# An attention stage over graph edges: scores spread from two row halves of TensorE, zero-one matrices in bf16, denominator factors written in place by ScalarE

## The reference, cut to what matters

```python
q, k, v = (x @ Wq.T), (x @ Wk.T), (x @ Wv.T)          # each (N, H=8, C=16)
scores = einsum('ehc,ehc->eh', q[dst], k[src]) / sqrt(C) + edge_attr @ We.T
seg_max = segment_max(scores, dst)
ex = exp(scores - seg_max[dst])
denom = segment_sum(ex, dst)
out = segment_sum(v[src] * (ex / denom[dst])[:, :, None], dst)
```

## Time and profile before

| | us |
|---|---|
| median of 3 runs | 6932.62 (6927.31 to 6932.69) |
| profiled execution | 6936.31 |
| its span in the profile | 6934.5 |

### The profile page before, as it was taken

How to read it: one execution, slowest core, us unless ns; L and a number is a source line. 1 busy time by engine, 2 the same in 40 slices (tenths; PEclk the granted TensorE clock), 3 DMA queues, 4 the chain that set the end, 5 groups by cost and what they waited for, 6 DMA issues and landing times. The chain is left out here.

```text
span 6934.5 us, 161023 instructions
## 1 busy us (share of the span) xinstructions
PE 5765.9 (83%) x49778; PEld 3934.9 (57%) x49778; DVE 4671.8 (67%) x15150; ACT 2162.6 (31%) x5294; POOL 3099.4 (45%) x3151
## 2 busy tenths in 40 slices
PE   4699999999998999984566659999889999599996
PEld 2466666666666666663344436666456666366664
DVE  7455555555555555558999967777557777577776
ACT  3222222222222222223333323333443333433332
POOL 1555555555555555547000025555145555355552
PEclk9655555555555555555556679999999999799997
DMA  4333333333333333324222233333343333533335
GB/s 145 116 89 87 88 87 88 88 88 89 87 87 87 88 89 86 89 70 131 86 66 70 65 115 105 106 103 104 102 128 104 104 105 101 163 104 106 106 102 152
DMA packets 542000, 688.39 MB, mean 99 GB/s; under 512 B 217072, under 2 KB 427905, under 8 KB 541722
## 3 DMA queue, kind: packets, MB, share of 16 engines
q0 software_dynamic: 140208, 338.71, 17.1%
q1 hardware_dynamic: 401692, 348.45, 16.6%
HBM read 619.25 MB, written 67.52 MB: 99 GB/s over the span
## 5 line engine op out<-in xcount | busy, mean ns | idle before, releaser
L740 POOL DMA_INDIRECT at_kv<-kv_tab,at_idx x1568 | 1562.2, 996 | 1296.6 <-issue 593.6
L2250 ACT ACTIVATE ag_msg<-ag_pair 128x768 bf16<-128x768 f32 x1200 | 925.9, 808 | 1586.4 <-PE ag_pair L2180 1027.1
L2189 PE MATMUL ag_sum<-ag_hot,ag_msg 128*128 128x240 bf16 x10800 | 1300.5, 268 | 69.6 <-issue 55.5
L2189 PEld LDWEIGHTS ag_sum<-ag_hot,ag_msg 128*128 128x128 bf16 x10800 | 974.6, 98 | 443.3 <-issue 366.6
L2064 POOL DMA_INDIRECT ag_spill<-g_tab,ag_idx x600 | 580.1, 967 | 1429.5 <-DMA ag_idx<-spill_tab 777.8
L2119 DVE CAST ag_msg<-ag_pair 128x768 bf16<-128x768 f32 x600 | 572.9, 955 | 588.8 <-PE ag_pair L2180 277.2
L2180 PE MATMUL ag_pair<-xs,ag_pick 128*32 128x384 bf16 x14400 | 821.3, 331 | 153.4 <-DVE ag_pick L2092 63.0
L2071 POOL DMA_INDIRECT ag_spill<-g_tab,ag_idx x750 | 724.5, 966 | 462.3 <-issue 179.1
L2102 DVE TENSOR_SCALAR ag_hot<-iota_win,ag_node 128x240 bf16<-128x240 bf16 x4350 | 901.2, 290 | 0.0
L989 PE MATMUL at_ps_bc<-at_sct,at_sel_head 64*128 64x128 f32 x3136 | 696.8, 408 | 33.9 <-issue 8.2
L989 PEld LDWEIGHTS at_ps_bc<-at_sct,at_sel_head 64*128 64x128 f32 x3136 | 639.2, 308 | 52.0 <-ACT at_sct L1059 41.1
(11 more groups left out here) (331 smaller groups left out, 9093.9 us busy)
## 6 DMA issues: line engine op xcount, KB each, us to landing
ag_pick<-slot_tab SPq DMA_DIRECT2D x150, 768.0 KB
rk_hi_bc<-hi_tab SPq DMA_DIRECT2D x50, 896.0 KB
at_attr<-attr SPq DMA_DIRECT2D x196, 128.0 KB
at_qd<-q_tab SPq DMA_DIRECT2D x1568, 12.0 KB
at_kv<-kv_tab,at_idx POOLq DMA_INDIRECT x1568
ag_spill<-g_tab,ag_idx POOLq DMA_INDIRECT x1350
tr_dv<-dinv_tab SPq DMA_DIRECT2D x72, 256.0 KB
g_tab<-xs SPq DMA_DIRECT2D x48, 384.0 KB
```

The lines of the kernel that those rows point to most:

```text
L740: nc.gpsimd.indirect_dma_start(kv[:, s.slot, ch, :], None, env["kv_tab"], bass.IndirectOffsetOnAxis(ap=idx[:, s.slot, ch:ch + 1], axis=0)) ...
L2189: last = nc.tensor.matmul(sum_ps[k][:, 0:WIN], row[:, part * DIM:(part + 1) * DIM], hot[:, k, ch, :], start=first and part == 0, stop=end ...
L2250: nc.scalar.activation(msg[:, p % 4, :, :], pair_ps[p % 3][:, :, 0:3 * DIM], ACT.Copy).then_inc(copied[p], 1)
```

## The change

- spread_scores: the turned scores (sct) are now on all 128 partitions, twice the same 64 rows. The heads 0 to 3 are spread from partitions 0 to 63 into ps_bc[0], the heads 4 to 7 from partitions 64 to 127 into ps_bc[1], with the matmuls of the two halves in turn (tile_position row 0 and row 64). Still 8 float32 matmuls. sel_head changes its shape accordingly and is made with two affine_selects.
- turn_scores: the transpose becomes two float32 matmuls with the identity, whose results go to partitions 0 to 63 and 64 to 127.
- bf16: hot, big_c, low_row and ones_row are made in bf16. place stays float32, and ScalarE makes a copy place_b in bf16 (cast_place). turn_hot and turn_place become bf16 matmuls with a bf16 identity (ident16); two of the three matmuls of near_max are bf16.
- denominators: sa_ps and its matmul are gone. ScalarE computes the same exponential a second time, directly into partitions 64 to 71 of scale_d (row 72 stays 1.0), and shrink reads that.
- order: on VectorE place_one and hot_one stand ahead of messages and fall_short, place_one first; on TensorE turn_hot and turn_place stand ahead of sum_up; on ScalarE cast_place stands between copy_scores and gain_exp. New waits: place_cast in near_max and turn_place, den_scale_made in shrink, scaled (of the block before) in scale_exp.

```diff
--- before.py
+++ after.py
@@ -583,13 +583,13 @@
...
         identb = tile("identb", [P, P], BF16)
-        sel_head = tile("sel_head", [C * HEADS, HEADS, P])
+        sel_head = tile("sel_head", [P, HALF, P])
         sel_feat = tile("sel_feat", [HEADS, HC, HEADS])
-        sel_aux = tile("sel_aux", [HEADS + 1, HEADS + 1])
         we = tile("we", [P, G * HEADS])
-        big_c = tile("big_c", [P, HEADS, C])
-        low_row = tile("low_row", [1, HEADS * C])
-        ones_row = tile("ones_row", [1, P])
+        ident16 = tile("ident16", [P, P], BF16)
+        big_c = tile("big_c", [P, HEADS, C], BF16)
+        low_row = tile("low_row", [1, HEADS * C], BF16)
+        ones_row = tile("ones_row", [1, P], BF16)
         turn, wrap, step = tile("turn", [P, 1]), tile("wrap", [P, 1]), tile("step", [P, 1])
@@ -598,18 +598,19 @@
...
 
-        hot = tile("hot", [P, SLOTS, P])
+        hot = tile("hot", [P, SLOTS, P], BF16)
         hot_w = tile("hot_w", [P, SLOTS, C * GAP + W])
...
         place = tile("place", [P, SLOTS, P])
+        place_b = tile("place_b", [P, SLOTS, P], BF16)
         place_t = tile("place_t", [P, SLOTS, P])
...
         sc = tile("sc", [P, SLOTS, C * HEADS])
-        sct = tile("sct", [C * HEADS, 2, P])
+        sct = tile("sct", [P, 2, P])
         ml = tile("ml", [P, HEADS])
@@ -619,7 +620,8 @@
...
         fall = tile("fall", [HEADS, P])
-        scale = tile("scale", [HEADS + 1, P])
+        scale = tile("scale", [HEADS, P])
+        scale_d = tile("scale_d", [P, P])
         m_node = tile("m_node", [P, HEADS])
@@ -631,9 +633,9 @@
...
         mt_ps, back_ps, mbt_ps = ps_max[:, 64:72], ps_max[:, 72:80], ps_max[0:HEADS, 128:256]
-        sf_ps, sa_ps = ps_scale[:, 0:128], ps_scale[AUXD:AUXROWS, 128:256]
+        sf_ps = ps_scale[:, 0:128]
         me_ps, bias_ps = ps_scale[:, 384:448], ps_scale[:, 448:512]
-        hot_ps, place_ps, sct_ps = ps_turn[:, 0:128], ps_turn[:, 128:256], ps_turn[0:C * HEADS, 256:384]
+        hot_ps, place_ps, sct_ps = ps_turn[:, 0:128], ps_turn[:, 128:256], ps_turn[:, 256:384]
         num_ps, den_ps = ps_node[:, 256:384], ps_node[AUXD:AUXROWS, 384:512]
...
@@ -692,22 +695,23 @@
...
             nc.gpsimd.memset(sel_feat[:, :, :], 0.0).then_inc(made, 1)
-            nc.gpsimd.memset(sel_aux[:, :], 0.0).then_inc(made, 1)
             nc.gpsimd.memset(hot_w[:, :, :], 0.0).then_inc(made, 1)
-            nc.gpsimd.memset(scale[:, :], 1.0).then_inc(made, 1)
+            nc.gpsimd.memset(scale_d[:, :], 1.0).then_inc(made, 1)
             nc.gpsimd.memset(msg[:, :, :, MSG - 1:MSG], 1.0).then_inc(made, 1)
...
             nc.gpsimd.memset(turn[:, :], 0.0).then_inc(made, 1)
-            pool.wait_ge(made, 11)
-            nc.gpsimd.affine_select(out=sel_head[:, :, :].rearrange("p h (c w) -> p h c w", w=W),
-                                    in_=sel_head[:, :, :].rearrange("p h (c w) -> p h c w", w=W),
-                                    compare_op=ALU.not_equal, fill=1.0, base=0,
-                                    pattern=[[-1, HEADS], [-HEADS, C], [0, W]], channel_multiplier=1).then_inc(made, 1)
+            pool.wait_ge(made, 10)
+            for j in range(2):
+                pool.wait_ge(made, 10 + j)
+                nc.gpsimd.affine_select(out=sel_head[:, :, :].rearrange("p h (c w) -> p h c w", w=W),
+                                        in_=sel_head[:, :, :].rearrange("p h (c w) -> p h c w", w=W),
+                                        compare_op=ALU.not_equal, fill=1.0, base=-(C * HEADS + HALF) * j,
+                                        pattern=[[-1, HALF], [-HEADS, C], [0, W]], channel_multiplier=1
+                                        ).then_inc(made, 1)
             nc.gpsimd.affine_select(out=sel_feat[:, :, :], in_=sel_feat[:, :, :], compare_op=ALU.not_equal, fill=1.0,
                                     base=0, pattern=[[0, HC], [-1, HEADS]], channel_multiplier=1).then_inc(made, 1)
-            nc.gpsimd.affine_select(out=sel_aux[:, :], in_=sel_aux[:, :], compare_op=ALU.not_equal, fill=1.0, base=0,
-                                    pattern=[[-1, HEADS + 1]], channel_multiplier=1).then_inc(made, 1)
+            nc.gpsimd.tensor_copy(ident16[:, :], ident[:, :]).then_inc(made, 1)
             nc.gpsimd.tensor_scalar(identb[:, :], ident[:, :], BIG, None, ALU.mult).then_inc(made, 1)
@@ -864,12 +868,13 @@
...
                     dve.wait_ge(scale_spread, s.nth)
+                    dve.wait_ge(den_scale_made, s.nth)
                     if not (isinstance(s.n, int) and s.n < 1):
...
                     nc.vector.tensor_tensor(num, num, sf_ps, ALU.mult).then_inc(scaled, 1)
-                    nc.vector.tensor_tensor(den, den, sa_ps, ALU.mult).then_inc(scaled, 1)
+                    nc.vector.tensor_tensor(den, den, scale_d[AUXD:AUXROWS, :], ALU.mult).then_inc(scaled, 1)
 
@@ -882,8 +887,8 @@
...
                     (4, scale_nodes), (4, load_bases), (3, node_max), (2, add_up), (3, load_first), (4, shrink),
-                    (3, raise_max), (2, add_bias), (4, merge), (3, messages), (3, fall_short), (0, hot_one),
-                    (0, place_one)], w)
+                    (3, raise_max), (2, add_bias), (4, merge), (0, place_one), (0, hot_one),
+                    (3, messages), (3, fall_short)], w)
                 dve.wait_ge(added, 2 * (w + 1) * sh.BLOCKS)
@@ -911,9 +916,8 @@
...
                     pe.wait_ge(above_made, s.nth if isinstance(s.n, int) and s.n == sh.BLOCKS - 1 else s.nth + 1)
-                    nc.tensor.matmul(sf_ps, sel_feat[:, :, :].rearrange("h d e -> h (d e)"), scale[0:HEADS, :], start=True, stop=True)
-                    nc.tensor.matmul(sa_ps, sel_aux[:, :], scale[:, :], start=True, stop=True,
-                                     tile_position=(0, AUXD)).then_inc(scale_spread, 1)
+                    nc.tensor.matmul(sf_ps, sel_feat[:, :, :].rearrange("h d e -> h (d e)"), scale[:, :], start=True,
+                                     stop=True).then_inc(scale_spread, 1)
 
@@ -923,9 +927,10 @@
...
                     pe.wait_ge(place_made, s.nth)
+                    pe.wait_ge(place_cast, s.nth)
                     nc.tensor.matmul(near_ps, ones_row[:, :], low_row[:, :].rearrange("p (h c) -> p h c", h=HEADS),
                                      start=True, stop=False, skip_group_check=True)
-                    nc.tensor.matmul(near_ps, place[:, s.slot, :], big_c[:, :, :], start=False, stop=False,
+                    nc.tensor.matmul(near_ps, place_b[:, s.slot, :], big_c[:, :, :], start=False, stop=False,
                                      skip_group_check=True)
@@ -966,7 +971,11 @@
...
                     alone(pe)
-                    nc.tensor.transpose(sct_ps, sc[:, s.slot, :], ident[:, :]).then_inc(sc_turned, 1)
+                    for j in range(2):
+                        at = slice(C * HEADS * j, C * HEADS * (j + 1))
+                        last = nc.tensor.matmul(sct_ps[at, :], sc[:, s.slot, :], ident[:, :], start=True, stop=True,
+                                                tile_position=(0, C * HEADS * j))
+                    last.then_inc(sc_turned, 1)
 
@@ -982,26 +991,28 @@
...
 
-                def spread_scores(j):
-                    def run(s):
-                        pe.wait_ge(sct_made, s.nth)
-                        for h in range(HALF):
-                            last = nc.tensor.matmul(ps_bc[j][:, h * P:(h + 1) * P], sel_head[:, HALF * j + h, :],
-                                                    sct[:, s.slot % 2, :], start=False, stop=h == HALF - 1,
-                                                    skip_group_check=True)
-                        last.then_inc(bc_made[j], 1)
-                    return run
+                def spread_scores(s):
+                    pe.wait_ge(sct_made, s.nth)
+                    for h in range(HALF):
+                        for j in range(2):
+                            own = slice(C * HEADS * j, C * HEADS * (j + 1))
+                            last = nc.tensor.matmul(ps_bc[j][:, h * P:(h + 1) * P], sel_head[own, h, :],
+                                                    sct[own, s.slot % 2, :], start=False, stop=h == HALF - 1,
+                                                    skip_group_check=True, tile_position=(C * HEADS * j, 0))
+                            if h == HALF - 1:
+                                last.then_inc(bc_made[j], 1)
 
...
                     alone(pe)
-                    nc.tensor.transpose(hot_ps, hot[:, s.slot, :], ident[:, :]).then_inc(hot_turned, 1)
+                    nc.tensor.matmul(hot_ps, hot[:, s.slot, :], ident16[:, :], start=True, stop=True).then_inc(hot_turned, 1)
 
                 def turn_place(s):
-                    pe.wait_ge(place_made, s.nth)
-                    nc.tensor.transpose(place_ps, place[:, s.slot, :], ident[:, :]).then_inc(place_turned, 1)
+                    pe.wait_ge(place_cast, s.nth)
```

(18 more changed lines are left out.)

7 lines of the change are left out of this document (4 added, 3 removed).

## The result

The changed kernel takes 6853.52 us (median of 4 runs, 6851.56 to 6858.99) against 6931.14 us for the kernel before (4 runs, 6927.31 to 6932.69): ratio 0.989, 95% interval 0.9873 to 0.9907, 78 us less. Forecast were 6550 us and a range of 6390 to 6800: the direction held, the size was off by 300 us, and the time lies outside the range.

A forecast was written before the change was run, and what follows sets the result against it. TensorE's queue was taken to set the 14.92 us block; edits saving 2.52 gave 12.40, plus 0.90 for a late signal, less 0.6 for the clock, 12.70 us per block. Forecast 6550 us, range 6390 to 6800.

The forecast's parts named there:

- Spreading: Spreading the scores on TensorE: products of the two row halves run side by side, gain 1.71 of 3.72 us per block.
- rival D: Row halves do not run beside each other in float32: 13.85 us per block, 6774 us; 9%.
- near_max: TensorE's near_max products: two go from two float32 records each to one bf16 record, gain 0.55 us (0.4 to 0.8).
- The turns: turn_hot and turn_place on TensorE: one bf16 record each, gain 0.1 us per block (-0.2 to 0.3).
- turn_scores: Transpose of the scores on TensorE becomes two float32 products in four records, costing 0.36 us per block (0.2 to 0.6).
- The held signal: Back-to-back gathers delay turn_near's signal to VectorE's raise_max, adding 0.9 us per block (0.4 to 1.07).
- The clock: TensorE's denser work brings more rises of its clock, saving 0.6 us per block (0 to 1.5).
- Rival C: TensorE's clock stays high for most of the stage and gathers bind at 10.6 us per block, 6137 us; 7%.
- rival E: A second late signal per block costs another 0.9 us: 14.2 us per block, 6843 us; 8%.
- Rival F: Slower: the signal of spreading itself is also late, by 1.8 us: 15.1 us per block, 7019 us; 6%.

The follow-up runs named there:

- e1: The changed kernel with four gathers per block instead of eight, part of the attention left out; 6372.08 us, 0.9273 of the kernel before.
- e7: The kernel before without its pace() line, so eight gathers stand back to back; 6268.63 us against 6262.31 for the kernel before, ratio 1.0006.
- e12: The changed kernel with scores transposed and spread from one row half as before; 6755.76 us against 6932.08 for the kernel before, ratio 0.9747.
- e15: The changed kernel with scores transposed and spread from one row half as before; 6088.15 us against 6263.72 for the kernel before, ratio 0.9724.
- e9: The changed kernel as it is, run again; 6853.99 us where the kernel before takes 6932.08, ratio 0.9887.
- e5: The changed kernel as it is, run again; 5959.45 us where the kernel before takes 6262.31, ratio 0.9513.

## Why the prediction was wrong, point by point

**Which edits are worth what: right.** The sum said 12.40 us of TensorE per undisturbed block; e1's block shows 11.98. Spreading 2.01 us (forecast 2.01), so the row halves run side by side in float32 with their weight loads, and rival D is out. near_max 0.97 us, in e1 0.80 (forecast 1.1). L915 is gone. The turns 0.32 us from L1010 to sum_up at 1505.15 (forecast 0.38). turn_scores 0.82 us to its copy (forecast about 0.75). Most of what the block is shorter than forecast is near_max, whose gain was forecast too small. The Trainium skill ("TensorEngine Tiling (Array Packing)", Key Properties) says that different tiles load weights and multiply in parallel; the 16 records in 2.01 us agree, now for float32 too.

**The held signal: the step that failed.** It was in the sum at 0.9 us per block, as a signal of turn_near, whose reader has slack; with the clock's 0.6 taken off, 0.3 us were to be added to TensorE's own work. Measured are 14.24 - 11.98 = 2.26 us. The term was too small because it had the wrong products in it. With the block shorter the bias and turn_max came into the run, and more of spreading. Readers that started over 1 us later than is usual in their kernel, between 500 and 2300 us, counted on the first engine record that reads the product:

| product | before | the change |
|---|---|---|
| turn_near | 21 of 123 | 27 of 126 |
| bias | 6 of 123 | 71 of 127 |
| turn_max | 6 of 123 | 57 of 127 |
| spreading (starts of run_max) | 47 of 246 | 116 of 254 |
| spread_max | 25 of 122 | 4 of 126 |

I had placed the run by events up to L958 and not asked which product stands next in TensorE's queue if the run lasts six gathers, not five. turn_near, the product that I had in the sum, hardly changed.

What held signals cost in all can be read from the two kinds of groups, the program of a row being the same (of before, e7 stands in for the free group, as it is as fast as before there):

| | held group, block | free group, block | difference |
|---|---|---|---|
| before | 14.66 | 12.57 (e7) | 2.09 |
| one row half | 13.71 (e12) | 11.54 (e15) | 2.17 |
| the change | 14.23 (e9) | 11.00 (e5) | 3.23 |

So the edits are worth 12.57 - 11.00 = 1.57 us per block, 306 us, in a free group, and in a held one 3.23 - 2.09 = 1.14 of it is lost. What is left is 0.43 us, 84 us: the measured gain. The row halves alone give 11.54 - 11.00 = 0.54 us and lose 3.23 - 2.17 = 1.06. These differences hold the waits and the lost rises of the clock together; the runs do not part them.

**The clock: wrong, and bound up with the held signals.** I expected more rises and 0.6 us per block from them. The granted clock stayed at 0.56 (before 0.57). Where nothing is held it is higher for both kernels. The totals of 600 to 2300 us, first e5 (the change), then e7 (before without pace()), the granted clock third from the end:

```profile
600.00:2300.00 1700.00, 1534.74 (x10159) 970.97 (x10158) 1260.97 (x3230) 609.96 (x2461) 1261.29 (x1234) 0.67 0.42 116
...
600.00:2300.00 1700.00, 1621.35 (x9064) 1144.75 (x9064) 1146.39 (x2843) 456.72 (x1894) 1052.96 (x1081) 0.65 0.37 102
```

The same stretch shows 0.57 for both kernels in a held group. In e7 there are two kinds of block and no other: 78 of 143 take 10.5 to 10.7 us, with 6.8 us of it at the raised clock, and 65 take 14.9 at the lower level. Before, in the held group, has 17 short ones of 123, and 41 of over 16 us. So most of what the free group gives the kernel before comes through the clock: my estimate is 1.7 of the 2.09 us, the share of short blocks rising from 14 to 55% at 4.3 us each. And the 0.26 us that I took for the net worth of a rise was the worth with held signals behind it. The change itself did little to the clock, 0.65 to 0.67 in the free groups. Rival C needed the transposes, turned into products, to raise the clock. The Trainium skill ("TensorE: Matmul & The Clock Gate", Part 4) says that a transpose does not count as busy in the way that products do; three per block were turned here, and neither pair of clocks (0.57 and 0.57 held, 0.65 and 0.67 free) shows much of it, though no run turned them alone.

**The rivals.** Nearest came rival E (14.2 us per block, 6843 us), a second held signal per block; it had 8%. That its number fits is in part luck: a held bias came in 71 of 127 blocks, mostly 1.8 to 2.2 us late, and such blocks are 2.1 us longer than the others; it is not 0.9 in every one. Rival F, the sign turned, did not come as a whole, though its mechanism did: starts of run_max, which reads the products of spreading, were late in 116 of 254 cases. And for the row halves alone F's outcome is true in the held group where both ran: with them 6853.99, without them 6755.76.

**The range.** Its upper end took in E only in part. The price for a held signal was taken from one row on a product with slack, and its frequency from one run of gathers. The bound that the rows would have allowed is the full delay on a product without slack, 2.42 - 0.60 = 1.82 us: 12.40 + 1.82 = 14.2 us, or 6842 us, which a range of 6390 to 6860 would have taken in. That it meets the measured 14.24 so closely is luck, as that is a mean of 15.12 and 13.01 over blocks with and without a held bias.

**What stays open.** Why the signals are held in some groups and not in others; the same chip showed both. It is a matter of the whole program, not of attention alone. Ahead of the first block both kinds take the same (216 us in the change's profile, 217 in e5), and so do the first 1000 us behind the last block, in which no gather runs. The three aggregations, in which GpSimd gathers again, take 811.5, 809.4 and 813.1 us from the first to the last of their main products (L2208) in the held profile, and 721.8, 722.3 and 723.2 in e5; 267 us less, which covers the difference outside the blocks (4077 us against 3814). VectorE's reader of TensorE's ag_pair there, the change first, then e5:

```profile
L2138 DVE CAST ag_msg<-ag_pair 128x768 bf16<-128x768 f32 x600 | 573.4, 956 | 590.4 <-PE ag_pair L2199 279.7
...
L2138 DVE CAST ag_msg<-ag_pair 128x768 bf16<-128x768 f32 x600 | 571.9, 953 | 141.4 <-PE ag_pair L2199 133.6
```

Of the 590 us the profile lays only 280 to the product; much of the rest it gives to DMAs such as tr_dv<-dinv_tab (149 us), not to "remote". Where this reader waited, it started 1.55 us behind the product's last record in the median, and 0.38 in e5. So held signals seem to cost the convolutions some 263 us as well; no run changed the gathers there. Open is also what decides which signal is hit: in e12 GpSimd spends even more of the time on gathers (1218 of 2000 us, the change 1152) and holds much less.
